# Thirty transposing SBUF-to-SBUF transfers in two blocks of an attention kernel

## The reference, cut to what matters

```python
q = (query @ Wq + bq).reshape(B, L, NKV, G, HDIM)
k_, v_ = jnp.split(kv @ Wkv + bkv, 2, axis=-1)
scores = jnp.einsum('blkgd,bmkd->bkglm', q, k) * scale
attn = jax.nn.softmax(scores, axis=-1)
o = jnp.einsum('bkglm,bmkd->blkgd', attn, v).reshape(B, L, NHEAD * HDIM)
return o @ Wo + bo
# and for the quantized block
w = NF4[codes]
w = w.reshape(O, I // BLOCK, BLOCK) * scales[:, :, None]
```

## Time and profile before

| | |
|---|---|
| median of 2 runs | 1011.77 us (1010.63 to 1012.92) |
| the profiled execution | 1011.92 us, of which the span of the trace is 1010.1 us |
| PE (TensorE) busy | 995.1 us, 99% of the span |
| DVE (VectorE), ACT (ScalarE), POOL (GpSimd) busy | 745.5, 586.5 and 443.5 us |
| DMA | 149.59 MB, mean 148 GB/s |

### The profile page before, as it was taken

One profiled execution on the slowest core, in us unless ns is written; L12 is line 12 of the kernel. 1 busy time (PEld: TensorE's weight loads), 2 busy tenths in 40 slices (PEclk: granted clock), 3 DMA queues, 4 the chain that ended last, 5 costly groups with the idle time before them and its releaser, 6 DMA issues.

```text
span 1010.1 us, 20355 instructions
## 1 busy us (share of the span) xinstructions
PE 995.1 (99%) x7083; PEld 921.6 (91%) x7083; DVE 745.5 (74%) x1680; ACT 586.5 (58%) x1254; POOL 443.5 (44%) x641
## 2 busy tenths in 40 slices
PE   8999999999999999999999999999999999999998
PEld 6779999999999999999999999999999999999744
DVE  5678878777777778777776778777777768676766
ACT  6466666666565656566565666656565655565431
POOL 2244553545534444345454444534444445333331
PEclk9999999999999999999999999999999999999999
DMA  9663333333324343243333334333333237464895
GB/s 324 226 223 130 124 129 132 109 134 108 124 94 134 119 135 135 96 134 108 131 106 116 114 132 137 116 119 108 130 107 134 97 124 249 158 223 153 235 351 166
DMA packets 90086, 149.59 MB, mean 148 GB/s; under 512 B 10529, under 2 KB 44977, under 8 KB 89985
## 3 DMA queue, kind: packets, MB, share of 16 engines
q1 hardware_dynamic: 88224, 146.42, 43.8%
q10 hardware_dynamic: 1424, 1.51, 0.4%
q0 software_dynamic: 336, 0.35, 0.2%
HBM read 82.97 MB, written 14.81 MB: 97 GB/s over the span
## 4 chain that ended last, share of the span: by engine, by line
PE 93%; DVE 3%; DMA 2%; issue 1%; SPq 0%; ACT 0%; DVEq 0%
PE p_kv L88 16%; PE p_kv L90 16%; PE p_kv L89 16%; PE p_s L88 7%; PE p_s L90 7%; PE p_s L89 6%; PE p_t L769 6%; PE p_o L88 5%; PE p_o L90 5%; PE p_o L89 5%; PE p_s L849 1%; PE p_ot L753 1%; DMA wkv_raw<-in_wkv 1%; PE p_o L783 1%; DMA probs_r<-probs 1%
## 5 line engine op out<-in xcount | busy, mean ns | idle before, releaser
L610 POOL TENSOR_SCALAR slots<-code 128x512 f32<-128x512 bf16 x232 | 148.7, 641 | 247.3 <-DVE slots L1466 162.4
L1210 ACT ACTIVATE pt_hi<-p_t 128x512 fp32r<-128x512 f32 x224 | 109.9, 542 | 113.6 <-PE p_t L769 107.9
L1466 DVE TENSOR_TENSOR slots<-slots 128x512 f32<-128x512 f32 x232 | 170.0, 733 | 1.6 <-POOL slots L610 1.5
L1239 ACT ACTIVATE slots<-code,drop_and_offsets 128x512 f32<-128x512 bf16 x232 | 158.6, 713 | 8.1 <-POOL code L606 4.1
L1198 ACT ACTIVATE v_hi<-p_kv 128x256 fp32r<-128x256 f32 x196 | 75.2, 384 | 139.6 <-PE p_kv L90 138.7
L630 POOL TENSOR_TENSOR slots<-slots 128x512 f32<-128x512 f32 x58 | 77.0, 1327 | 158.2 <-DVE slots L1466 158.2
L1430 DVE TENSOR_TENSOR pt_lo<-p_t,pt_hi 128x512 fp32r<-128x512 f32 x224 | 128.7, 614 | 5.9 <-ACT pt_hi L1210 4.9
L1415 DVE TENSOR_TENSOR v_lo<-p_kv,v_hi 128x256 fp32r<-128x256 f32 x196 | 83.1, 424 | 67.6 <-ACT v_hi L1198 64.8
L88 PE MATMUL p_kv<-wkv_hi,ctx_even_hi 128*128 128x256 f32 x448 | 129.1, 288 | 0.2 <-DVE v_lo L1415 0.2
L89 PE MATMUL p_kv<-wkv_lo,ctx_even_hi 128*128 128x256 f32 x448 | 126.0, 281 | 0.0
L90 PE MATMUL p_kv<-wkv_hi,ctx_even_lo 128*128 128x256 f32 x448 | 126.0, 281 | 0.0
(11 more groups left out here) (261 smaller groups left out, 2717.7 us busy)
## 6 DMA issues: line engine op xcount, KB each, us to landing
probs_r<-probs SPq DMA_DIRECT2D x110, 448.0 KB, 3.6
code<-in_codes SPq DMA_DIRECT2D x58, 256.0 KB, 3.8
scale<-in_scales SPq DMA_DIRECT2D x114, 128.0 KB, 3.1
expanded_weights<-slots SPq DMA_DIRECT2D x56, 256.0 KB, 2.1
ctx_st<-in_ctx_t SPq DMA_DIRECT2D x96, 112.0 KB, 3.0
ring_hi<-expanded_weights SPq DMA_DIRECT2D x22, 256.0 KB, 5.9
ring_lo<-expanded_weights SPq DMA_DIRECT2D x22, 256.0 KB, 6.0
wq_hi<-in_wq SPq DMA_DIRECT2D x4, 1024.0 KB, 7.2
```

The source lines that it names most:

```text
L610: nc.gpsimd.tensor_scalar(slots[:, slot, :], code16[:], LINES[j][0], LINES[j][1], ALU.mult, ALU.add).then_inc(pool_lines, 1)
L1210: nc.scalar.activation(pt_hi[:, at:at + n, :].rearrange("p t q -> p (t q)"), p_t[:, c % 2, 0:n * ROWS], ACT.Copy).then_inc(pt_rounded, 1)
L1239: nc.scalar.activation(slots[:, slot, :], code16[:], ACT.Identity, bias=offsets[:, k:k + 1], scale=LINES[j][0]).then_inc(act_lines, 1)
L1466: nc.vector.tensor_tensor(slots[:, slot, :], slots[:, slot, :], slots[:, other, :], ALU.max).then_inc(merged, 1)
```

## The change: what it does

In blocks 24 and 26 SyncE, right after the two moves of `probs`, waits until both have landed and until the codes of tile i+1 have been narrowed, and then issues transposing DMAs from `code16` (128 x 512, two bytes each) into the space of `probs`, seen as 28 tiles of 128 x 128 two-byte elements, of which 24 are written. In block 24 these are 24 transfers of one 128 x 128 tile (32 KB) each. In block 26 they are 6 transfers of four such tiles (128 KB) each. Nothing reads the result. VectorE's first write of `probs` in the following block waits for them, and so does the next narrowing of codes on GpSimd that would overwrite `code16`. `code16` is also allocated ahead of four small tiles and no longer behind them.

```diff
+        code16 = sb(st, "code16", [P, TW], BF16)
+        codes_t = probs[:].rearrange("p r c -> p (r c)").bitcast(BF16).rearrange("p (t q) -> p t q", q=P)
+        codes_turned = sem("codes_turned")
+        TURNED, TURNS_OF = (3 * NKV, 3 * NKV + 2), (16 * 24, 16 * 6)
...
-        code16 = sb(st, "code16", [P, TW], BF16)
...
+                if i in TURNED:
+                    turn_codes(i)
+
+            def turn_codes(i):
+
+                sp.wait_ge(code_narrow, i + 2)
+                sp.wait_ge(probs_moved, 32 * (i + 1))
+                if i == TURNED[0]:
+                    for t in range(24):
+                        sp.dma_start(codes_t[:, t], code16[:, t % 4 * P:(t % 4 + 1) * P], transpose=True).then_inc(codes_turned, 16)
+                else:
+                    for t in range(0, 24, 4):
+                        sp.dma_start(codes_t[:, t:t + 4], code16[:], transpose=True).then_inc(codes_turned, 16)
...
+                if n - 2 in TURNED:
+                    wait_apart(pool, codes_turned, sum(TURNS_OF[:TURNED.index(n - 2) + 1]), pool_passed)
                 nc.gpsimd.tensor_copy(code16[:], code[:]).then_inc(code_narrow, 1)
...
                 if i > 0:
                     dve.wait_ge(probs_moved, 32 * i)
+                if i - 1 in TURNED:
+                    dve.wait_ge(codes_turned, sum(TURNS_OF[:TURNED.index(i - 1) + 1]))
```

## The result

The changed kernel takes **1051.64 us** (median of 2 runs, 1050.65 to 1052.63) against 1011.77 us before; the ratio is 1.0394, with a 95% interval of 1.0328 to 1.0460. It is slower by 39.9 us. The prediction was 1055 us in a range of 1028 to 1105.

What follows compares the result with a forecast made beforehand. TensorE, busy 99% of the span, was taken as the bound. Context delays of 1.6 + 24x + 6z = 40.6 us plus 3 us of restart, 43.6 over 1011.92, gave 1055 us, range 1028 to 1105.

Steps and rivals of the forecast that it cites:

- 0.8 + 24x: Block 24: predicted TensorE delay in us from the late second context piece, after 2.1 us of room.
- 24x - 0.8: Block 24: smaller delay in us from the first context piece, through the keys; not added to the second's.
- x: Block 24: price of one single-tile transposing transfer on SyncE's queue, taken as 1.0 us.
- z: Block 26: price of one four-tile transposing transfer on SyncE's queue, taken as 2.5 us.
- the main case: Blocks 24 and 26: x from 0.7 to 1.3, z from 1.2 to 4; 1036 to 1075 us, chance 0.55.
- Rival A: Blocks 24 and 26: price goes by the tile, z = 4x; 1064 us at x = 1.0, 1079 at 1.3; chance 0.23.
- Rival B: SyncE's queue takes the transfers like ordinary ones, x = 0.42 and z = 0.58; not slower, 1027 us; chance 0.12.
- C: Blocks 24 and 26: each transfer finishes before the next, x = 1.9 and z = 7.6; 1110 us, chance 0.06.
- D: Blocks 24 and 26: transfers written element by element in two-byte packets; about 2340 us, chance 0.03.
- E: Whole kernel: cost hidden or kernel faster; against it, the landing wait alone costs 0.8 us a block; chance 0.01.
- The wait on VectorE: VectorE's wait for the transfers before writing `probs`: 24x - 4.8 us, within the context delay, so costed at nothing.
- The restart: TensorE after its two long stops: slower first matmuls, 0 to 2.6 us each, taken as 1.5, 3 in all.

Runs made afterwards that it cites:

- The waits alone: The changed kernel without its transposing transfers and the VectorE and GpSimd waits on them; SyncE still waits for the moved probabilities: 1011.25 us, ratio 0.9996.
- the pair of spread kernels: The changed kernel with twelve four-tile transfers, three in each of blocks 24 to 27: behind context pieces 1013.79 us, at the change's own place 1029.12 us.
- the plain transfers: The changed kernel with its thirty transfers issued as plain copies of the same bytes, without transposition: 1033.95 us, ratio 1.0212.
- the kernels with four and eight tiles a transfer: The changed kernel with block 24's 24 transfers replaced by six of four tiles (1030.24 us) or three of eight (1026.52 us).
- the context first: The changed kernel with the transposing transfers of both blocks issued behind the two context pieces and ahead of the weight tile: 1047.73 us, ratio 1.0351.
- the last experiment: The changed kernel with twelve four-tile transfers, three in each of blocks 24 to 27, ahead of codes and context pieces: 1029.12 us, ratio 1.0167.

## Why the prediction was right, point by point

**The bound and the path: right.** TensorE had no room, the list of SyncE held the context back behind the transposing transfers, ScalarE stood in front of its rounding, and TensorE stopped. The waits alone and the pair of spread kernels show both halves of it.

**The formula: its other branch was right.** I let the second context piece set the delay (0.8 + 24x) and set the first aside (24x - 0.8). With the measured 24x = 31.61 these give 32.4 and 30.8 us; TensorE waited 30.02, at the place of the first, and nowhere after it. I had put the second piece 7.7 us behind the last transfer; ScalarE rounded it at 472.25, 6.6 us behind. It was awaited by ScalarE for 2.27 us, and TensorE did not feel it. TensorE worked at the lower clock until about 475 us and so reached the turned probabilities later, which fits, but no run separates the two. In block 26 the first branch, 6z - 0.8, gives 7.1 us, and 6.51 were measured; for the plain transfers it gives 15.8, and 15.2 were measured.

**The two prices: both mis-sized, and they cancelled.** x was taken as 1.0 and measured 1.32 us: 31.6 us where I had 24. z was taken as 2.5 and measured 1.32: 7.9 where I had 15. The sum of both came to 39.5 against my 39. That the total is right to 3 us is partly this luck. The reason behind z, that a transfer of four tiles lies between one and four times the price of one, is wrong: the price is per instruction, from one to eight tiles. "If x comes out near z" was one of the prediction's own signs of failing, and it came out so, 1.32 and 1.32: on how the price grows with the size the prediction failed by its own measure, though the time is right. For x the right order came from bounds of 0.42 and 1.9, and only that; 1.32 lies at the edge of the 0.7 to 1.3 on which the main case was counted.

**Two small slips in the working.** The span of 1036 to 1075 us for the main case is not quite its sum: 1.6 + 24x + 6z with 0 to 5.2 us of restart gives 1037.5 to 1073.9. And "every ordinary issue in these rows" is below 0.62 us only by the medians; the earlier trace rows has one of 1.354. Neither moves the forecast.

**Rival A,** the price by the tile, is refuted by block 26 itself and by the kernels with four and eight tiles a transfer. The Trainium skill's 1309 ns for a 128 x 128 two-byte transpose by DMA (VectorE: DVE Perf Modes, "The three transpose paths") agrees with 1.32 us a transfer in block 24; read as a price of each tile it does not agree with block 26, where four tiles cost the same.

**Rival B,** the price of an ordinary transfer: refuted, 1.32 against 0.69 us (16.57 / 24) for the same bytes unturned. The statement in Advanced Engine Details and Errata of the Trainium skill, "X-Bar Transpose (TRN2)", that transposing transfers are as fast as regular ones, does not hold here for the issue, which doubles; the landing is 2.4 against 1.8 us. C (1.9 us each, one after another) did not come: transfers landed 2.4 us after an issue and were issued every 1.32 us, so they overlapped. Nor did D (single elements): the changed kernel moved 7103 packets more than the kernel before (97189 against 90086), not 16384 for each of 48 tiles. E (hidden or faster) did not come either, though the 0.8 us a block that its paragraph counts for the wait for the landing did not show: the waits alone cost nothing that can be measured.

**The wait on VectorE at nothing: right,** and without the late context it does cost, as predicted: 27.2 us of TensorE's time in block 25, where 24x - 4.8 gives 26.9 with x = 1.32. That the numbers meet so closely is luck in part. With the context first, the transfers began at 437.79, some 3 us later than where the formula starts them (7.2 us after the moves were issued and not 4.2). Against this the 24 took 30.65 us and not 31.6, and they landed sooner: I had counted 1.9 us from the end of the last issue, and it was 2.3 from its start.

**The restart: right in size,** 3 us predicted, 3.6 measured, but from rows that do not show it. The first matmuls of the program, from which it was taken, were slow at a granted clock of 1.00:

```profile
5.00:7.00 2.00, 2.00 (x6) 1.55 (x6) 1.00 1.05 397
```

Behind the two stops of the change the granted clock was 0.50. So the term met its size by luck, and what it stood for was another thing.

## What to carry to other kernels

Count a transposing SBUF-to-SBUF DMA by its instructions, not by its bytes: 1.3 us of the issuing queue each here, for up to the eight tiles tried, so put several tiles into one. Nothing in this kernel reads what the transfers wrote; these runs say what they cost, and nothing of the order in which a transfer of several tiles writes them. Then ask what stands behind it in that queue and how late each of those may come; the same twelve transfers cost 17 us ahead of a context load and 2 us behind it. When one late transfer is moved out of the way, look at once for the wait that it covered.

## What was unexpected in the hardware

- Single issues took 0.5 to 1.3 us longer than their neighbours: the third of the 24 in the change 2.34 against 1.23 us, the fifth of the plain ones 1.90 against 0.60, the third of eight tiles 1.99 against 1.36. It is not the first use of a form: in the last experiment the third issue of each of the four blocks took 1.81, 2.29, 2.23 and 1.82 us. Nor does it always come: with the context first none of the 24 took more than 1.34, and in block 26 of the change none of the six more than 1.36. The cause is open.
- Short stops can cost clock as well as long ones. After a stop of about 3 us TensorE fell to the lower level as it did after 30 us, and behind the last experiment's stop of 2.4 us the granted clock was 0.50 as well (at 470 to 472 us). TensorE's busy time rose by 5 us over the four stops of that experiment, more than the 3.6 us after the change's two.
